# Two strips of heads on TensorE, scores two groups at a time, q's stacked copies held back, low parts on VectorE, in a cross-attention and MoE block

## The chip, the cores and the metric

The kernel runs on one core of one Trainium2 chip. The metric is the device time of one execution in microseconds (us), taken as the median of a few executions.

## The reference

Sixteen batch elements of 128 tokens, width 128. Cut to what matters:

```python
x = x + attention(layernorm(x), ctx, ctx)       # 16 heads of 8 dimensions
x = x + moe(layernorm(x))
# attention: q, k, v = projections with biases
scores = q @ k.T / sqrt(8) + m[h] * softplus(1000 + |i - j|)     # a slope m per head
out    = softmax(scores) @ v, then the projection Wo and its bias
# moe: router softmax over 16 experts, top 2; gated experts of 64 features and a shared one of 128
y = sum_e c_e * (silu(x @ Wg_e) * (x @ Wu_e)) @ Wd_e + shared(x)
```

## The kernel before

**Tiling.** Work goes by groups of two batch elements (b = 0, 1), eight groups in all (NG = 8). Everything of a group has its tokens in 128 partitions or its features there. TensorE, ScalarE, VectorE and GpSimd each have their own instruction order, written out by hand, with semaphores between them; SyncE issues most DMAs.

**Stages.** `first()` does the attention of group 0. Then come seven steps, `step(f, a, p, q, abuf)`: the experts of group f, the attention of group a = f+1, the q and k projections of p = f+2 and the first norm of q = f+3. Steps 1 to 4 are a loop. Each step has a first part and a `second_half`. The experts of the last group stand behind the steps. Inside a step, pieces of the two halves are interleaved: nine chunks `up(f, c)` (six products each), nine chunks `late_down` of the group before, the scores and the values.

**Stacked heads.** To have near-float32 scores from float16 products, q and k are each split into a high float16 part and a low one (`qk_parts`). ScalarE writes the high part (`qk_high`, L714), then a full float32 copy (`qk_copy`, L718); GpSimd subtracts the two (`qk_low`, L1308). In group 0 VectorE makes the low part straight from PSUM instead (`qk_low_first`, L949). SyncE writes the parts to DRAM (L217 to L221) and reads them back as stacks (L229, L235): for each head, 32 rows of `stacks_sb` hold k's and q's parts so that one product over them gives high x high, high x low and low x high together. Rows 96 and 97 hold the shift (below) against ones. The rows between are zeros, filled at the start (L1182, L1195 on VectorE, L860 on ScalarE). A product of scores takes 96 rows, one of transposed scores 98.

**Scores and the shift.** Heads go in four groups g of four, one PSUM bank each. `scores(a, b, g)` (L360) fills the bank `ps_s[g % 2]`; VectorE takes each row's largest value per head (`row_max`, L966), splits it into float16 halves (`nsplit`, L972, L976); TensorE turns it (`shift_T`, L369), ScalarE copies it (`nmT`, L724) and issues the small DMA that writes it into the q stack (`shift_rows`, L741). `scores_T(a, b, g)` (L415) then gives transposed scores minus the maximum in `ps_st`, ScalarE takes the exponential (L730), and `weigh_values` (L434) multiplies by the values. The bias of the slopes is either a product of `dist16` with slope matrices (L378, L383) or a copy of `bias_T` put in the bank ahead (`seed_first` on ScalarE, L737; `seed` on VectorE, L985).

**Which waits matter.** `scores` waits for the maximum two groups back, `scores_T` for the exponential two groups back, and with b = 0 or 1 and g = 0 for the shift rows' DMA. `up(f, 0)` ends with two products on `x2_lo` (L1023 on VectorE, from `x2_hi` of ScalarE, L767). The lines of the change:

```python
# L355: pe.wait_ge(max_sb, n - 1)            scores: the maximum two groups back
# L406: pe.wait_ge(exp_sb, n - 1)            scores_T: the exponential two groups back
# ScalarE, a step: norm2(f,1) qk_high(p,1) x2_high(f) qk_copy(p,1) qk_high(p,0) tanh(f,0) qk_copy(p,0) ...
#   ... tanh(f,3) exponential(a,0,0) shift_copy(a,1) shift_rows(a,1) exponential(a,0,1) tanh(f,4) ...
# VectorE, a step: row_max 0, 1; gate, hidden (f-1, 8); x2_low(f); row_max 2, 3; max_high; gate(f,0); max_low ...
```

Of the kernel before, what the change touches and what calls it, by code (L numbers as in the profile page):

```python
# [17 lines left out]
F32 = mybir.dt.float32  # L18
# [7 lines left out]
P = 128  # L26
# [14 lines left out]
SMALL_SLOPES = 4  # L41
SROWS = 4 * DH
ZROWS = 96
AROWS = ZROWS + 2
# [24 lines left out]
def xattn_moe_kernel(nc, x, ctxT, wqkvoT, bqk, bv, bo, wgT, wuT, wd, wr, c_ident, c_dist, c_select, out):  # L69
# [8 lines left out]
    with stack:  # L78
# [35 lines left out]
        qk_parts, qk_full = sb("qk_parts", [P, 2, 2, T], F16), sb("qk_full", [P, 2, T])  # L114
        stacks_sb = sb("stacks_sb", [AROWS, 2, 2, H, T], F16)
# [5 lines left out]
        nsplit = sb("nsplit", [P, NB, 2, H], F16)  # L121
# [33 lines left out]
        ps_pv = psum("ps_pv", [P, 512])  # L155
        ps_up = [psum("ps_up0", [P, 2, T]), psum("ps_up1", [P, 2, T])]
# [37 lines left out]
        qkfull_sb = sem("qkfull_sb")  # L194
# [15 lines left out]
        def _(sp):  # L210
            def stacks(p, buf):
# [10 lines left out]
                if at_start(p):  # L222
                    sp.wait_ge(act_pads, 1)
                elif isinstance(p, int) and p == 1:
                    sp.wait_ge(dve_pads, 2)
                sp.wait_ge(s_kd, 32 * p + 32)
                for plane, row in ((2, 0), (3, 2 * DH)):
                    src = bass.AP(qk_dram.tensor, (buf * 5 + plane) * (P * T), [[H * T, 2 * DH], [1, H * T]])
                    sp.dma_start(stacks_sb[row:row + 2 * DH, buf, 1].rearrange("r h t -> r (h t)"), src).then_inc(s_stack, 16)  # L229
                if at_start(p):  # L230
                    sp.wait_ge(dve_pads, 1)
# [20 lines left out]
            def load_more():  # L252
                sp.wait_ge(s_nm[0], 16)
                sp.wait_ge(s_nm[1], 16)
                sp.dma_start(x_all[:, 2 * NB:4 * NB, :], x[:, 2 * NB:4 * NB, :]).then_inc(s_x, 16)
                sp.dma_start(ctx_all[:, 2 * T:4 * T], ctxT[:, 2 * T:4 * T]).then_inc(s_ctx, 16)

            def load_rest():
                sp.wait_ge(s_stack, 128)
# [3 lines left out]
                sp.wait_ge(dve_pads, 3)  # L263
# [30 lines left out]
        def _(pe):  # L294
# [42 lines left out]
            def scores(a, b, g, buf):  # L337

                bank, n = ps_s[g % 2], 2 * NHG * a + NHG * b + g
                if b == 0 and g == 0:
                    pe.wait_ge(s_stack, 64 * a + 64)
                    if at_start(a):
# [3 lines left out]
                        pe.wait_ge(dve_pads, 1)  # L348
                        pe.wait_ge(act_pads, 1)
                    elif isinstance(a, int) and a == 1:  # L350
                        pe.wait_ge(act_pads, 3)
                elif b == 0 and g == 1:
                    pe.wait_ge(v_sb, a + 1)
                else:
                    pe.wait_ge(max_sb, n - 1)  # L355
                if g == 0:
                    mm(bank[:], dist16[:], slope_hi[:, 0:HG, :], start=True, stop=False, skip_group_check=True)
                for h in range(HG * g, HG * g + HG):
                    o = (h - HG * g) * P
                    last = mm(bank[:, o:o + P], qs[buf][0:ZROWS, h, b * P:(b + 1) * P],  # L360
                              ks[buf][0:ZROWS, h, b * P:(b + 1) * P],
                              start=(g > 0), stop=True, skip_group_check=True)
                last.then_inc(s_mm, 1)
# [243 lines left out]
            def second_half(f, a, p, q, abuf):  # L607
# [5 lines left out]
                if not at_start(f): down(f - 1, (8,), abuf)  # L613
# [784 lines left out]
```

## Time and profile before

| | |
|---|---|
| median of 3 runs | 248.25 us (247.99 to 249.17) |
| profiled execution | 249.56 us, its span 247.8 us |
| busy: TensorE products, weight loads | 216.5 us, 177.5 us |
| busy: VectorE, ScalarE, GpSimd | 172.4 us, 124.9 us, 83.4 us |
| granted TensorE clock | full, but for 0.67 on average from 27 to 42.5 us |

The times add to more than the span since the engines work side by side. The profiled execution is 249.56 us long by the device's clock, 1.8 us more than its span. A step starts at 42.25, 66.35, then about every 26 us; the steps end at about 226 us.

### The profile page before, as it was taken

How to read it: one execution, taken by the hardware profiler on the slowest of the kernel's cores; microseconds unless marked ns; L12 is line 12 of the kernel's file. 1: busy time of each engine (PE TensorE's matmuls, PEld its weight loads, DVE VectorE, ACT ScalarE, POOL GpSimd, SP SyncE). 2: the span in 40 equal slices, each digit the busy share in tenths (PEclk: the TensorE clock that was granted, in tenths of full speed). 3: DMA queues.
4: the chain of work that ended last, by engine and by line, in shares of the span. 5: the costliest groups of instructions: out<-in, count | busy, mean ns of one | idle time of the engine just before them, and what ended most of it. 6: DMA issues, size and time to landing. Idle time of an engine off the chain costs nothing.

```text
span 247.8 us, 6092 instructions
## 1 busy us (share of the span) xinstructions
PE 216.5 (87%) x1937; PEld 177.5 (72%) x1937; DVE 172.4 (70%) x600; ACT 124.9 (50%) x298; POOL 83.4 (34%) x192
## 2 busy tenths in 40 slices
PE   2978588878989698989999899979997989989995
PEld 2666346666779577967798688957895779768985
DVE  4689614796789556993698478856885589654882
ACT  8475543656454545356446534655545424644320
POOL 2501012501483118610791059114830182018100
PEclk9999957999999999999999999999999999999999
DMA  5553582163303460156106510734044500170000
GB/s 152 169 90 118 107 296 79 36 105 101 75 3 98 69 173 0 42 105 162 31 3 138 144 48 1 136 91 105 3 116 90 132 1 4 26 171 0 0 25 21
DMA packets 13079, 20.24 MB, mean 82 GB/s; under 512 B 2800, under 2 KB 9440, under 8 KB 12544
## 3 DMA queue, kind: packets, MB, share of 16 engines
q1 hardware_dynamic: 12080, 18.64, 31.3%
q10 hardware_dynamic: 976, 1.32, 1.9%
q8 instruction: 12, 0.20, 0.3%
q14 instruction: 11, 0.09, 0.1%
HBM read 16.03 MB, written 3.78 MB: 80 GB/s over the span
## 4 chain that ended last, share of the span: by engine, by line
PE 35%; issue 32%; POOL 13%; DMA 7%; DVE 6%; ACT 5%; ACTq 0%; POOLq 0%; SPq 0%; DVEq 0%
PE ps_up L501 7%; POOL hid L1315 6%; PE ps_m L527 6%; DMA stacks_sb<-nmT 6%; PE ps_pv L434 4%; PE ps_up L506 3%; PE ps_pv L441 2%; PE ps_st L415 2%; DVE nmax L966 2%; PE ps_s L360 2%; DVE stacks_sb L1195 1%; DMA ident<-in_c_ident 1%; POOL qk_parts L1308 1%; PE ps_st L469 1%; PE ps_m L456 1%
## 5 line engine op out<-in xcount | busy, mean ns | idle before, releaser
L730 ACT ACTIVATE probs<-ps_st 128x512 f32<-128x512 f32 x64 | 37.8, 594 | 27.4 <-PE ps_st L415 27.2
L786 ACT ACTIVATE th<-ps_up 128x256 f32<-128x256 f32 x72 | 27.6, 383 | 35.6 <-PE ps_up L506 35.4
L527 PE MATMUL ps_m<-wd_sb,hid 128*128 128x128 f32 x288 | 44.2, 281 | 0.0
L1070 DVE SCALAR_TENSOR_TENSOR tg<-th,ps_up 128x256 f32<-128x256 f32 x72 | 29.8, 414 | 20.2 <-ACT th L786 19.7
L966 DVE TENSOR_REDUCE nmax<-ps_s 128x4 f32<-128x512 f32 x64 | 41.9, 679 | 0.5 <-issue 0.4
L1315 POOL TENSOR_TENSOR hid<-hid,crep 128x256 f32<-128x256 f32 x56 | 39.0, 729 | 5.2 <-ACT x2n L760 3.4
L527 PEld LDWEIGHTS ps_m<-wd_sb,hid 128*128 128x128 f32 x288 | 37.7, 191 | 0.6
L415 PE MATMUL ps_st<-stacks_sb 98*128 98x128 f16 x256 | 25.7, 225 | 9.5 <-DMA stacks_sb<-nmT 6.7
L1076 DVE TENSOR_TENSOR hid<-tg,ps_up 128x256 f32<-128x256 f32 x72 | 29.7, 412 | 1.0
L1271 POOL TENSOR_TENSOR ve<-mv,eps_sb 128x1 f32<-128x1 f32 x16 | 3.0, 189 | 79.6 <-DVE mv L1017 79.6
L415 PEld LDWEIGHTS ps_st<-stacks_sb 98*128 98x128 f16 x256 | 17.9, 100 | 15.6 <-DVE ps_st L985 6.3
L501 PE MATMUL ps_up<-x_hi,wg_hi 128*128 128x256 f32 x72 | 26.6, 369 | 2.5 <-ACT x_hi L767 2.4
L360 PE MATMUL ps_s<-stacks_sb 96*128 96x128 f16 x256 | 23.7, 219 | 0.7 <-DVE nmax L966 0.7
L360 PEld LDWEIGHTS ps_s<-stacks_sb 96*128 96x128 f16 x256 | 17.8, 98 | 4.6 <-DVE nmax L966 1.6
L506 PE MATMUL ps_up<-x_lo,wg_hi 128*128 128x256 f32 x72 | 20.3, 282 | 0.0
L501 PE MATMUL ps_up<-x_hi,wu_hi 128*128 128x256 f32 x72 | 20.3, 282 | 0.0
L501 PE MATMUL ps_up<-x_hi,wu_lo 128*128 128x256 f32 x72 | 20.3, 282 | 0.0
L501 PE MATMUL ps_up<-x_hi,wg_lo 128*128 128x256 f32 x72 | 20.2, 280 | 0.0
L506 PE MATMUL ps_up<-x_lo,wu_hi 128*128 128x256 f32 x72 | 20.1, 280 | 0.0
L434 PE MATMUL ps_pv<-probs,v_aug 128*32 128x384 f32 (+1 forms) x256 | 18.9, 416 | 0.5 <-ACT probs L730 0.5
L1263 POOL TENSOR_TENSOR ve<-mv,eps_sb 128x2 f32<-128x2 f32 x8 | 1.6, 194 | 46.6 <-DVE mv L934 46.6
L501 PEld LDWEIGHTS ps_up<-x_hi,wg_hi 128*128 128x128 f32 x72 | 13.7, 190 | 4.8 <-issue 1.9
(149 smaller groups left out, 447.4 us busy)
## 6 DMA issues: line engine op xcount, KB each, us to landing
crep<-cw_dram SPq DMA_DIRECT2D x28, 256.0 KB, 4.4
stacks_sb<-qk_dram SPq DMA_DIRECT2D x32, 128.0 KB, 4.0
qk_dram<-qk_parts SPq DMA_DIRECT2D x16, 128.0 KB, 1.8
out_y<-x_all SPq DMA_DIRECT2D x8, 128.0 KB, 4.4
wg_sb<-in_wgT ACTq DMA_DIRECT2D x1, 576.0 KB, 3.5
wu_sb<-in_wuT ACTq DMA_DIRECT2D x1, 576.0 KB, 3.3
wd_sb<-in_wd SPq DMA_DIRECT2D x1, 576.0 KB, 4.7
x_all<-in_x SPq DMA_DIRECT2D x2, 256.0 KB, 3.5
```

The costliest lines, as they stand in the source:

```text
L360: last = mm(bank[:, o:o + P], qs[buf][0:ZROWS, h, b * P:(b + 1) * P], ks[buf][0:ZROWS, h, b * P:(b + 1) * P], start=(g > 0), stop=True, sk ...
L415: last = mm(bank[:, o:o + P], ks[buf][:, h, b * P:(b + 1) * P], qs[buf][:, h, b * P:(b + 1) * P], start=first, stop=True, skip_group_check ...
L434: last = mm(ps_pv[32 * c:32 * c + 32, r * 3 * P:(r * 3 + n) * P], v_aug[:, b, r, c, :], probs[:, b, h * P:(h + n) * P], start=True, stop=T ...
L501: mm(ps_up[c % 2][:, k, :], w[:, c, :], x2_hi[:], start=(k == 0 and n == 0), stop=False, skip_group_check=True)
L506: last = mm(ps_up[c % 2][:, k, :], hi[:, c, :], x2_lo[:], start=False, stop=True, skip_group_check=True)
L527: last = mm(ps_dn[:, b * P:(b + 1) * P], hid[:, buf, c, b * P:(b + 1) * P], wd_sb[:, c, :], start=(c == 0 and b == 0), stop=(c == SHARED), ...
L730: fn(probs[:, b, g * HG * P:(g + 1) * HG * P], ps_st[(g + 1) % 2][:], ACT.Exp).then_inc(exp_sb, 1)
L786: fn(th[:, c % 2, :], ps_up[c % 2][:, 0, :], ACT.Tanh, scale=0.5).then_inc(tanh_sb, 1)
L966: v.tensor_reduce(nmax[:, b, HG * g:HG * g + HG], ps_s[g % 2][:].rearrange("p (h j) -> p h j", h=HG), AX_X, ALU.max, negate=True).then_inc ...
L1070: v.scalar_tensor_tensor(out=tg[:, c % 2, :], in0=th[:, c % 2, :], scalar=1.0, in1=ps_up[c % 2][:, 0, :], op0=ALU.add, op1=ALU.mult).then_ ...
L1076: v.tensor_tensor(hid[:, buf, c, :], tg[:, c % 2, :], ps_up[c % 2][:, 1, :], ALU.mult).then_inc(hid_sb, 1)
L1315: g.tensor_tensor(hid[:, buf, c, :], hid[:, buf, c, :], crep[:, c, :], ALU.mult).then_inc(hc_sb, 1)
```

## The change

- **Strips.** The stack has two strips of rows, 0 to 33 and 64 to 97: heads 0 to 7 in the first, heads 8 to 15 in the second. There are no rows of zeros and so no fills. A product of scores takes 32 rows, one of transposed scores 34.
- **Pairs.** A call of `scores` or `scores_T` does two groups of heads, one from each strip, in alternation, into the two banks. It waits for both banks (maximum or exponential `n`, not `n - 1`). The order of groups is 0, 2, 1, 3.
- **Seeds.** In group 0 all biases of `scores_T` are products; later one seed on ScalarE and two on VectorE, all into one bank.
- **Low parts.** `qk_copy` and GpSimd's `qk_low` go; VectorE makes the low parts from PSUM, around `x2_low`, and waits until both high parts are there.
- **DMAs.** Each stack copy and each copy of shift rows is two DMAs, one per strip. SyncE waits for the shift rows of b = 1 before it issues q's stack copies.
- **Order.** `down(f-1, 2)` stands ahead of `up(f, 0)`, `down(f-1, 8)` behind the values of b = 0; ScalarE's copy of the values stands behind two exponentials; GpSimd doesn't wait for `x2n` before it weighs experts.

```diff
 # rows
+STRIP = 64
-ZROWS = 96
-AROWS = ZROWS + 2
+AROWS = SROWS + 2
+HS = H // 2
+ORDER = (0, 2, 1, 3)
 # SyncE, stacks(p)
                 sp.wait_ge(s_qd, 16 * p + 16)
+                if not at_start(p):
+
+                    sp.wait_ge(s_nm[1], 32 * p)
                 for row in (0, 2 * DH):
-                    src = bass.AP(qk_dram.tensor, buf * 5 * (P * T), [[H * T, 2 * DH], [1, H * T]])
-                    sp.dma_start(stacks_sb[row:row + 2 * DH, buf, 0].rearrange("r h t -> r (h t)"), src).then_inc(s_stack, 16)
+                    for s in range(2):
+                        src = bass.AP(qk_dram.tensor, (buf * 5 * P + s * HS) * T, [[H * T, 2 * DH], [1, HS * T]])
+                        at = STRIP * s + row
+                        sp.dma_start(stacks_sb[at:at + 2 * DH, buf, 0].rearrange("r h t -> r (h t)"), src).then_inc(s_stack, 16)
 # TensorE, scores(a, b, j)
+                    pe.wait_ge(max_sb, n)
+                for k in range(HG):
+                    for s in range(2):
+                        row, h = STRIP * s, HG * j + k
+                        last = mm(ps_s[s][:, k * P:(k + 1) * P], qs[buf][row:row + SROWS, h, b * P:(b + 1) * P],
+                                  ks[buf][row:row + SROWS, h, b * P:(b + 1) * P], start=(j > 0 or s > 0), stop=True,
+                                  skip_group_check=True)
+                        if k == HG - 1:
+                            last.then_inc(s_mm, 1)
 # TensorE, scores_T(a, b, j)
+                seeded = not at_start(a) and (b, j) != (0, 1)
...
+                if not (at_start(a) and b == 0 and j == 0):
+                    pe.wait_ge(exp_sb, n)
...
+                for k in range(HG):
+                    for s in range(2):
+                        row, h = STRIP * s, HG * j + k
+                        last = mm(scores_bank(a, 2 * j + s)[:, k * P:(k + 1) * P], ks[buf][row:row + AROWS, h, b * P:(b + 1) * P],
+                                  qs[buf][row:row + AROWS, h, b * P:(b + 1) * P], start=first[s], stop=True,
+                                  skip_group_check=True)
 # TensorE, a step
                 scores(a, 0, 0, abuf)
-                scores(a, 0, 1, abuf)
...
                 late_down(0)
-                scores(a, 0, 2, abuf)
                 late_down(1)
                 expert_in_T(f)
-                scores(a, 0, 3, abuf)
+                scores(a, 0, 1, abuf)
+                late_down(2)
                 up(f, 0)
-                late_down(2)
+                up(f, 1)
                 scores(a, 1, 0, abuf)
...
-                scores_T(a, 0, 0, abuf)
+                scores_T(a, 0, 0, abuf, f=f)
                 late_down(6)
                 shift_T(a, 1)
-                scores_T(a, 0, 1, abuf, f=f)
                 late_down(7)
...
                 up(f, 4)
-                scores_T(a, 0, 2, abuf)
+                scores_T(a, 0, 1, abuf)
                 weights_T(f, a)
-                scores_T(a, 0, 3, abuf)
                 up(f, 5)
-                if not at_start(f): down(f - 1, (8,), abuf)
                 scores_T(a, 1, 0, abuf)
                 weigh_values(a, 0, f)
+                if not at_start(f): down(f - 1, (8,), abuf)
                 scores_T(a, 1, 1, abuf)
                 values_T(a, 0)
-                scores_T(a, 1, 2, abuf)
 # TensorE, first()
+                scores_T(0, 0, 0, 0)
                 shift_T(0, 1)
-                keep_clock(2)
-                scores_T(0, 0, 0, 0)
                 scores_T(0, 0, 1, 0)
 # ScalarE
-                    act.wait_ge(qkfull_sb, 2 * p)
+                    act.wait_ge(qklo_sb, 2 * p + 2)
...
                 act.wait_ge(nm_sb, 2 * a + b + 1)
-                act.dma_start(qs[buf][ZROWS:AROWS, :, b * P:(b + 1) * P], nmT[:, b, :]).then_inc(s_nm[b], 16)
+                for s in range(2):
+                    act.dma_start(qs[buf][STRIP * s + SROWS:STRIP * s + AROWS, :, b * P:(b + 1) * P],
+                                  nmT[H * s:H * (s + 1), b, :]).then_inc(s_nm[b], 16)
 # ScalarE, a step
                 shift_copy(a, 1)
                 shift_rows(a, 1, abuf)
+                exponential(a, 0, 1)
...
                 exponential(a, 1, 0)
+                exponential(a, 1, 1)
                 values_copy(a, 0)
-                exponential(a, 1, 1)
 # VectorE
+            def qk_low(p, k):
+                if at_start(p):
+                    dve.wait_ge(qkhi_sb, 2 - k)
+                else:
+                    dve.wait_ge(qkhi_sb, 2 * p + 2)
...
+                bank = ps_k0 if k and at_start(p) else ps_qk[:, k * T:(k + 1) * T]
                 v.scalar_tensor_tensor(out=qk_parts[:, k, 1, :], in0=bank, scalar=bqk_sb[:, k:k + 1],
                                        in1=qk_parts[:, k, 0, :], op0=ALU.add, op1=ALU.subtract).then_inc(qklo_sb, 1)
 # VectorE, a step
+                if p is not None: qk_low(p, 1)
                 x2_low(f)
+                if p is not None: qk_low(p, 0)
                 row_max(a, 0, 2)
 # VectorE and ScalarE, at the start
-            v.memset(stacks_sb[:, 0, 0].bitcast(F32), 0.0).then_inc(dve_pads, 1)
-            v.memset(stacks_sb[:, 1].bitcast(F32), 0.0).then_inc(dve_pads, 1)
-            fill(stacks_sb[:, 0, 1], zero)
+            for s in range(2):
+                fill(ks[0][STRIP * s + SROWS:STRIP * s + AROWS], ones16)
 # GpSimd, a step
-                    pool.wait_ge(x2n_sb, NB * f + NB)
...
-                    qk_low(p, 1)
-                    qk_low(p, 0)
```

## Rows read from the trace of the kernel before

**Rows 1.** The page: its span and the busy time of each engine

```profile
span 247.8 us, 6092 instructions
...
PE 216.5 (87%) x1937; PEld 177.5 (72%) x1937; DVE 172.4 (70%) x600; ACT 124.9 (50%) x298; POOL 83.4 (34%) x192
```

**Rows 2.** The chain that ended last, step 3: start us, us, what

```profile
120.37 0.45 PE ps_s L360 x8
...
137.03 1.04 PE ps_pv L434 x16
```

**Rows 3.** TensorE in order of time, step 3, first part

```profile
123.89 0.38 PE L501 MATMUL ps_up<-x_hi,wg_hi 128*128 128x256 f32 x1 [0.41 <-ACT x_hi L767]
...
126.38 0.40 PE L360 MATMUL ps_s<-stacks_sb 96*128 96x128 f16 x4
126.71 0.23 PE L369 MATMUL ps_pv<-ident,nsplit 128*32 128x128 f16 x1
126.87 0.28 PE L469 MATMUL ps_st<-wr_hi,x_lo 128*128 128x16 f32 x1
```

**Rows 4.** VectorE in order of time: the start, and step 3

```profile
10.21 0.48 DVE L949 SCALAR_TENSOR_TENSOR qk_parts<-ps_st,bqk_sb,qk_parts 128x256 f16<-128x256 f32 x1 [1.20 <-ACT qk_parts L705]
...
12.90 3.47 DVE L1195 MEMSET stacks_sb<- 98x4096 f32 x1 [0.80 <-issue]
...
123.90 0.42 DVE L1023 TENSOR_TENSOR x_lo<-ps_st,x_hi 128x256 fp32r<-128x256 f32 x1 [0.51 <-ACT x_hi L767]
124.24 1.28 DVE L966 TENSOR_REDUCE nmax<-ps_s 128x4 f32<-128x512 f32 x2
```

**Rows 5.** ScalarE in order of time, step 3

```profile
123.38 0.38 ACT L767 ACTIVATE x_hi<-ps_st 128x256 fp32r<-128x256 f32 x1 [0.25 <-PE ps_st L462]
123.66 0.47 ACT L718 ACTIVATE qk_full<-ps_st,bqk_sb 128x256 f32<-128x256 f32 x1
...
132.05 0.27 ACT L724 ACTIVATE nmT<-ps_pv 32x128 f16<-32x128 f16 x1
132.35 0.62 ACTq L741 DMA_DIRECT2D stacks_sb<-nmT  x1
133.08 0.60 ACT L730 ACTIVATE probs<-ps_st 128x512 f32<-128x512 f32 x1 [0.77 <-PE ps_st L415]
...
134.87 0.36 ACT L779 ACTIVATE cwT<-ps_pv 16x256 f32<-16x256 f32 x1
```

**Rows 6.** TensorE in order of time: scores_T and what stands by it, four stages

```profile
27.12 0.40 PE L415 MATMUL ps_st<-stacks_sb 98*128 98x128 f16 x4 [1.35 <-ACT ps_st L737]
...
30.18 0.61 PE L415 MATMUL ps_st<-stacks_sb 98*128 98x128 f16 x4 [0.97 <-DVE ps_st L985]
...
52.95 0.38 PE L415 MATMUL ps_st<-stacks_sb 98*128 98x128 f16 x4 [1.22 <-DMA stacks_sb<-nmT]
...
57.28 0.40 PE L415 MATMUL ps_st<-stacks_sb 98*128 98x128 f16 x4 [0.38 <-DVE ps_st L985]
...
130.97 0.39 PE L415 MATMUL ps_st<-stacks_sb 98*128 98x128 f16 x4
...
131.78 0.23 PE L369 MATMUL ps_pv<-ident,nsplit 128*32 128x128 f16 x1
...
132.34 0.39 PE L415 MATMUL ps_st<-stacks_sb 98*128 98x128 f16 x4
...
136.65 0.38 PE L415 MATMUL ps_st<-stacks_sb 98*128 98x128 f16 x4 [0.66 <-DMA stacks_sb<-nmT]
...
145.75 0.38 PE L357 MATMUL ps_s<-slope_hi,dist 128*128 128x512 f16 x1
...
209.17 0.39 PE L415 MATMUL ps_st<-stacks_sb 98*128 98x128 f16 x4
...
214.14 0.40 PE L415 MATMUL ps_st<-stacks_sb 98*128 98x128 f16 x4
```

**Rows 7.** Waits over the whole run: us in total, times, longest us

```profile
PE ps_st L415 <- DMA stacks_sb<-nmT: 6.7, 6, 1.6
```

More of the change, by code:

```diff
@@ L335, in project_v, with scores @@
                 last.then_inc(v_mm, 1)
[L337 to L343, printed above, removed]
+            def scores(a, b, j, buf):
+                n = 2 * NHG * a + NHG * b + 2 * j
+                if b == 0 and j == 0:
+                    pe.wait_ge(s_stack, 128 * a + 128)
+                    pe.wait_ge(v_sb, a + 1)
                     if at_start(a):
@@ L347, in scores @@
                         pe.wait_ge(own, 6)
[L348 to L353, printed above, removed]
-                else:
[L355 to L363, printed above, removed]
+                else:
+                    pe.wait_ge(max_sb, n)
+                if j == 0:
+                    mm(ps_s[0][:], dist16[:], slope_hi[:, 0:HG, :], start=True, stop=False, skip_group_check=True)
+                for k in range(HG):
[6 more added lines that the diff above has]
+                            last.then_inc(s_mm, 1)
             def shift_T(a, b):
@@ L411, in scores_T @@
                         pe.wait_ge(act_pads, 2)
-                first = False if seeded else bias(bank, g)[0]
-                for h in range(HG * g, HG * g + HG):
-                    o = (h - HG * g) * P
-                    last = mm(bank[:, o:o + P], ks[buf][:, h, b * P:(b + 1) * P], qs[buf][:, h, b * P:(b + 1) * P],
-                              start=first, stop=True, skip_group_check=True)
-                    first = False
-                last.then_inc(st_mm, 1)
+                    elif isinstance(a, int) and a == 1:
+                        pe.wait_ge(act_pads, 4)
+                first = [False if seeded else bias(scores_bank(a, 2 * j), ORDER[2 * j])[0],
+                         bias(scores_bank(a, 2 * j + 1), ORDER[2 * j + 1])[0]]
+                for k in range(HG):
[4 more added lines that the diff above has]
+                                  skip_group_check=True)
+                        first[s] = False
+                        if k == HG - 1:
+                            last.then_inc(st_mm, 1)
             def weigh_values(a, b, f=None):
@@ L532, in first @@
                 scores(0, 0, 0, 0)
-                scores(0, 0, 1, 0)
                 keep_clock(1)
@@ L884, in _ @@
             fn(wr_hi[:], wr_sb[:], ACT.Copy).then_inc(act_setup, 1)
-            act.wait_ge(s_stack, 64)
+            act.wait_ge(s_stack, 128)
             act.dma_start(wu_sb[:], wuT).then_inc(s_wu, 16)
-            act.wait_ge(dve_pads, 2)
-            fill(ks[1][ZROWS:AROWS], ones16)
+            for s in range(2):
+                fill(ks[1][STRIP * s + SROWS:STRIP * s + AROWS], ones16)
             first()
@@ L1093, in first @@
                 max_low(0, 0)
-                for g in range(NHG):
-                    row_max(0, 1, g)
+                row_max(0, 1, 0)
+                row_max(0, 1, 1)
+                qk_low(1, 1)
+                qk_low(1, 0)
+                row_max(0, 1, 2)
+                row_max(0, 1, 3)
                 max_high(0, 1)
@@ L1138, in step @@
                 hidden(f, 2, 1 - abuf)
+                row_max(a, 1, 2)
                 row_max(a, 1, 3)
@@ L1158, in second_half @@
                 seed(a, 0)
-                seed(a, 1)
                 gate(f, 5)
@@ L1162, in second_half @@
                 hidden(f, 5, 1 - abuf)
+                seed(a, 1)
                 if not at_start(f): residual2(f - 1)
@@ L1342, in _ @@
             pool.wait_ge(zero_sb, 1)
-            inverse_deviation1(0)
+            step(None, None, None, 0, 0)
             pool.wait_ge(rstd1_sb, 1)
```

143 lines of the change are left out of this document (53 added, 90 removed).

## The prediction

> **What bounds the kernel now.** I read the page first: TensorE is busy for 216.5 of 247.8 us, the other engines far less [rows 1]. That makes it the first suspect, but a busy TensorE is not a full one, so I read its own order of time through step 3, and beside it those of VectorE and ScalarE in the same window. TensorE is in order; what counts is each place where it waits, and on whom. In a step there are few: for `x2_hi` ahead of the first `up` (0.41 us), and for the shift rows of b = 1 ahead of `scores_T(a, 1, 0)` (0.66) [rows 3, 6]. The wait list puts all waits of `scores_T` for that small DMA at 6.7 us in six times [rows 7]; 1.22 of it is in step 0 [rows 6], so steps 1 to 5 lose about 1.1 each. All the rest of a step is TensorE's own sequence. The change touches both: it packs products, and it rearranges what the waits hang on.
>
> **The pairs on TensorE.** Eight products of 96 rows take 0.45 us, 0.056 each, so four take 0.22 [rows 2]. If the two strips work side by side, a pair call has four slots: 0.22 instead of 0.45. That tiles can work side by side, the values show: 16 products on strips of 32 columns move 8 x 384 + 8 x 128 = 4096 columns in 1.04 us [rows 2], 0.25 ns a column in float32, where the untiled float16 products take 56/128 = 0.44. But a switch between tiled and untiled isn't free. `shift_T` is one product with 32 columns: the four ahead of it start at 126.38 and should be over at 126.60, it starts at 126.71, and what follows it starts at 126.87, 0.10 later than one product would need [rows 3]. So in and out cost 0.11 + 0.10 = 0.21, and a pair call is 0.43, against 0.45 now. All 8 calls of a step together win less than 0.2 us, in places where TensorE will wait anyway; I count 0. The bounds for strips of rows, which this trace doesn't show: no switch cost (a call is 0.22) and no overlap (0.66). I take 0.43, since strips of columns on this same engine are the nearest row for both.
>
> The Trainium skill's TensorEngine Tiling (Array Packing), Theoretical Speedup, has up to 2x for a dimension of at most 64, and its Key Properties say that changing the mode drains TensorE. The gaps by `shift_T` agree with the second; by the first alone, the eight calls of a step would save 8 x 0.22 = 1.8 us and seven steps 12.
>
> **First part of a step: VectorE gets later.** Now `x2_low` starts at 123.90, right behind `x2_hi`, and `row_max` 2 and 3 at 124.24 [rows 4]. With the change `qk_low(p, 1)` stands ahead of it and waits for both high parts; that of q is made on ScalarE only behind `x2_hi`, in the slot of the copy at 123.66, and takes 0.47: ready at 124.13 [rows 5]. `qk_low` at 0.48 [rows 4] (its group-0 form, the same operation) gives 124.6, `x2_low` at 0.42 is ready at 125.03, 0.7 later than today. The last two products of `up(f, 0)` need it. TensorE, which has filled its gap with `down(f-1, 2)` and so starts `up(f, 0)` near 123.95, stands some 0.5. The second `qk_low` (0.4 in sequence) puts `row_max` 2 and 3 at 125.35 to 126.6, 1.1 later. `scores(a, 1, 0)` needs both maxima now, TensorE waits again, then `shift_T(a, 0)` for the halves of the maximum: it comes near 127.4 instead of 126.71. From there to `scores_T(a, 0, 0)` the sequence is the same work, **+0.7 a step** where p exists (bounds: 0 if the two waits are absorbed, +1.1). What leaves GpSimd (two `qk_low`) and ScalarE (two copies) was hidden work: 0. That GpSimd weighs earlier lets `down(f-1, 2)` stand ahead of `up`: in this sum already.
>
> **Second part: a chain through ScalarE.** X is the start of `scores_T(a, 0, 0)`. Today the next exponential needs one bank, and TensorE runs ahead: `scores_T(a, 0, 2)` goes in without a wait. Now `scores_T(a, 0, 1)` needs both exponentials, and the second stands on ScalarE behind `shift_copy(a, 1)` and two DMA issues. Step by step: the call is 0.17 (a bias product of three heads) + 0.43; `down` 6 and `shift_T` follow as now, where `shift_T` is 131.78 - 130.97 - 0.22 = 0.6 behind its quad [rows 6], so it starts at X + 1.2; the copy starts 0.27 later (131.78 to 132.05) and takes 0.27, and one issue 0.62 [rows 5, 6]; two issues X + 3.0; the exponential waits out the issue, as at 133.08 (0.1), 0.6 [rows 5]: X + 3.7. Then `scores_T(a, 0, 1)`: bias 0.40 (131.94 to 132.34 [rows 6]), then the tiled products, 0.26 to their last start and some 0.25 to ScalarE; two exponentials of 0.57 and between them the weights' copy 0.3 (0.36 as recorded [rows 5]). So `scores_T(a, 1, 0)` can start at about **X + 6.1**. It waits for both exponentials as well. TensorE stands some 1.1 us before the first of them and 0.6 before the second; `up(f, 4)`, `up(f, 5)` and the weights' turning are its cover, and used up. Behind ScalarE's issues queue the exponential and `tanh(f, 4)`.
>
> Today that distance is 136.65 - 130.97 = 5.68 in step 3, and with the mean wait of 1.1 instead of 0.66 it is 6.1 in steps 1 to 5; 4.33 in step 0 (57.28 - 52.95) and 4.97 in step 6 (214.14 - 209.17) [rows 6, 7]. So holding back q's copies removes a wait for the DMA, and the chain takes its place: **0 in steps 1 to 5**. In step 0 there is no `down` 6, the chain is 5.6: **+1.3**. In step 6, **+1.1**. The second issue is bounded by 0 and 0.62 (each has half the rows to write); I take 0.62, its own line's.
>
> From `scores_T(a, 1, 0)` to the next step it is 9.1 us now (145.75 - 136.65) [rows 6]. `down(f-1, 8)` moves in (0.44), the values' wait for their copy goes (about 0.4), and the second seed, behind `gate`, `norm1` and `hidden`, holds `scores_T(a, 1, 1)` by some 0.2: +0.1. Held q copies start when the shift rows have landed and have 9 us until the next step: hidden. SyncE's `cw_dram` and `crep` issues queue behind them and come some 3 us later; their cover is the time to the next step's weighing.
>
> **The start.** The fills go, 3.47 us of it on VectorE [rows 4]. But it ran while the stacks were on their way, and pairs take turns with `row_max`: TensorE waits for two maxima, VectorE for two banks, some 0.6 between each two. That gives back what the fill frees: 0. Then today's four `scores_T` follow each other, 3.06 us from 27.12 to 30.18 [rows 6]. Now `shift_T(0, 1)` stands behind the first pair, and exponentials behind its copy and two issues: the chain as above without `down` and weights' copy, 5.2, with more bias products (all of group 0) 5.7. **+2.6**; the seed on ScalarE that goes (its end set 27.12) is about paid by the second issue for b = 0.
>
> **Sum.** Start 2.6; step 0: first part 0.5 (part of its 0.7 lies beside the 1.22 wait for the DMA) + 1.3 + 0.1 = 1.9; steps 1 to 5: 5 x (0.7 + 0 + 0.1) = 4.0; step 6: no `qk_low`, the moved `down` gives back 0.2, + 1.1 + 0.1 = 1.0. Together 9.5 us. The span is then 257.3. The profiled execution is at 249.56, 0.5% over the median of 248.25; on the median the sum gives **257.7 us**.
>
> **Rivals.**
> - *The hold pays (faster).* If the chain from X is short, the wait for shift rows is simply gone. TensorE's own work from X to `scores_T(a, 1, 0)` is 5.68 - 0.66 - 0.44 = 4.6 (less the wait there and the moved `down`). The chain stands in seven steps and the start, so each 0.1 of it is 0.8 in all; it decides from X + 4.9, 1.2 below my sum. At 4.6: 257.7 - 8 x 1.5 = **245.7 us**. For it: the DMA waits are real. Against it: exponential, issue and copy have measured lengths. 0.15.
> - *Row strips switch freely.* Five of the eight calls of a step lie on the path, each 0.2 shorter, 7.0 in seven steps, 0.6 at the start: **250 us** (247.5 to 252). Nothing in the trace speaks for it but that these are other strips than the values'. 0.2.
> - *No overlap.* Two strips, or their weight loads, go one after the other: + 0.22 in each of five to eight calls, 8 to 12 us: **268**. Against it: the values' strips overlap. 0.12. The skill's TensorE: Matmul & The Clock Gate, Measured speedup vs the span model, has 3.07x for four row strips at 512 columns; in proportion a pair would be 0.29 instead of 0.22, 2 to 4 us more than my sum. No row here shows it.
> - *My forecast* with its own bounds (second issue short: -4; first part 0 to 1.1): 252 to 262. 0.53.
>
> **Range and chances.** 247.5 to 265 leaves out the faster case and most of the slowest. A difference under 0.5% (1.2 us) is what a measurement of this kernel can't tell from none. Faster 0.15; within it half of the free switch, 0.1; slower 0.75.
>
> **What would show it.** After: `scores_T` pairs in 0.22 with gaps of 0.1 on both sides (free: no gaps; no overlap: 0.45); `x2_low` behind a `qk_low` near 1.1 us after `x2_hi` starts; waits of `scores_T` and its weight loads put down to exponentials instead of the DMA; two issues of 0.6 in a row on ScalarE; X to `scores_T(a, 1, 0)` near 6.1 in every step. The forecast is wrong if that distance is under 5, if `scores` pairs have no gaps, or if step 0's `scores_T(1, 0, 0)` comes before 55, two behind 52.95.

## The result, and the profile after

The changed kernel takes 263.2 us (262.35 to 264.45, 4 runs) against 248.71 us (4 runs): ratio 1.057, interval 1.050 to 1.065. It is slower by 14.5 us, the forecast had 9.5. Here and below, a ratio leaves out executions of either kernel that were disturbed, so it need not be the quotient of the two medians. Its profiled execution is at 262.74, with a span of 260.9. The page: span, TensorE's busy time, and TensorE's granted clock in 40 slices:

```profile
span 260.9 us, 6137 instructions
...
PE 222.8 (85%) x1946; PEld 166.1 (64%) x1946; DVE 174.2 (67%) x610; ACT 117.9 (45%) x284; POOL 74.2 (28%) x178
...
PEclk9999755685899999999999999999999999999999
```

TensorE is busy for 6 us more, the span is 13.1 us longer [rows 1]. The clock stands at 5 and 6 in several slices between 33 and 65 us. Two stretches of the windows view, after; the columns are length, busy time (instructions) of TensorE, its weight loads, VectorE, ScalarE and GpSimd, then the granted clock, DMA share and GB/s:

```profile
27.00:47.00 20.00, 13.84 (x86) 7.05 (x86) 4.20 (x20) 6.29 (x13) 2.17 (x6) 0.56 0.44 138
47.00:72.00 25.00, 22.43 (x176) 15.09 (x175) 17.36 (x61) 13.07 (x31) 3.23 (x10) 0.74 0.29 79
```

The same two of the kernel before:

```profile
27.00:47.00 20.00, 16.15 (x118) 10.40 (x118) 8.46 (x32) 9.97 (x22) 5.15 (x15) 0.74 0.46 136
47.00:72.00 25.00, 22.01 (x206) 17.75 (x207) 19.22 (x72) 13.75 (x36) 7.31 (x18) 1.00 0.34 78
```

So here is a difference that the prediction has no term for: a mean clock of 0.56 instead of 0.74, then 0.74 instead of 1.00. From 72 us on both run at 1.00.

TensorE in step 3, after, in order of time (start, us, engine, line, operation, count, and in brackets the idle time before it and who ended it):

```profile
129.62 0.39 PE L358 MATMUL ps_s<-slope_hi,dist 128*128 128x512 f16 x1
129.94 0.40 PE L362 MATMUL ps_s<-stacks_sb 32*128 32x128 f16 x8
130.27 0.70 PE L323 MATMUL ps_st<-xnT,wT 128*128 128x256 f32 x2
...
134.73 0.39 PE L518 MATMUL ps_up<-x_lo,wg_hi 128*128 128x256 f32 x1 [0.44 <-DVE x_lo L1015]
...
136.32 0.39 PE L358 MATMUL ps_s<-slope_hi,dist 128*128 128x512 f16 x1 [0.38 <-DVE nmax L957]
...
141.18 0.33 PE L386 MATMUL ps_st<-slope_small,dist 128*128 128x384 bf16 x1
...
145.02 0.34 PE L381 MATMUL ps_st<-slope_hi,dist 128*128 128x384 f16 x1 [1.02 <-ACT probs L720]
...
147.36 0.32 PE L386 MATMUL ps_st<-slope_small,dist 128*128 128x384 bf16 x1 [0.43 <-DVE ps_st L977]
...
156.39 0.38 PE L358 MATMUL ps_s<-slope_hi,dist 128*128 128x512 f16 x1
```

The pair of scores: bias at 129.62, eight tiled products from 129.94, next instruction 130.27. Narrow windows on this stretch show that the eight start in four couples, at 129.94, 130.01, 130.06 and 130.12, so a slot is 0.06 and the four are over near 130.18. The next instruction comes some 0.1 after that (the way out). From the start of the bias product to the next one it is 0.22 at 119.99 in the kernel before and 0.32 here, 0.1 more on the way in. The pair's 0.43 of the forecast is 0.43 to 0.44. In the first part of the step the wait for `x_lo` is 0.44, for the two maxima 0.38 (before: 0.41 for `x2_hi` [rows 3], and none for the maxima, at 125.16). In the second part X, the start of `scores_T(a, 0, 0)`, is 141.18; the second pair waits 1.02 for an exponential, the third pair (147.36) 0.43 for VectorE's seed. X to the third pair is 6.18 (forecast 6.1), where it was 5.68 [rows 6]; in step 6 it is 6.11, in step 0 6.96. The waits over the whole run say it in two lines:

```profile
PE ps_st L381 <- ACT probs L720: 11.9, 10, 2.8
...
PE ps_st L386 <- DVE ps_st L977: 2.6, 6, 0.4
```

No wait of `scores_T` for the DMA is left; 6.7 us of it were there [rows 7]. The chain took its place. VectorE in step 3, after, in order of time:

```profile
133.86 0.48 DVE L939 SCALAR_TENSOR_TENSOR qk_parts<-ps_st,bqk_sb,qk_parts 128x256 f16<-128x256 f32 x1 [0.94 <-ACT qk_parts L707]
134.26 0.41 DVE L1015 TENSOR_TENSOR x_lo<-ps_st,x_hi 128x256 fp32r<-128x256 f32 x1
134.60 0.47 DVE L939 SCALAR_TENSOR_TENSOR qk_parts<-ps_st,bqk_sb,qk_parts 128x256 f16<-128x256 f32 x1
134.99 1.28 DVE L957 TENSOR_REDUCE nmax<-ps_s 128x4 f32<-128x512 f32 x2
```

ScalarE in step 3, after, in order of time:

```profile
142.68 0.27 ACT L713 ACTIVATE nmT<-ps_pv 32x128 f16<-32x128 f16 x1
142.97 1.28 ACTq L732 DMA_DIRECT2D stacks_sb<-nmT  x2
144.36 0.60 ACT L720 ACTIVATE probs<-ps_st 128x512 f32<-128x512 f32 x1 [1.42 <-issue]
...
145.93 0.60 ACT L720 ACTIVATE probs<-ps_st 128x512 f32<-128x512 f32 x1 [0.70 <-PE ps_st L425]
```

`x_lo` comes behind a `qk_low` [rows 4], and two issues of the shift rows take 1.28 on ScalarE, one took 0.62 [rows 5]: the second costs full price, though each writes half the rows. The exponential waits them out.

The start on TensorE, after: the second, third and fourth pair, and the first product of step 0:

```profile
29.29 0.45 PE L381 MATMUL ps_st<-slope_hi,dist 128*128 128x384 f16 x1 [2.80 <-ACT probs L720]
...
31.89 0.61 PE L381 MATMUL ps_st<-slope_hi,dist 128*128 128x512 f16 x1 [1.17 <-ACT probs L720]
...
36.85 0.50 PE L381 MATMUL ps_st<-slope_hi,dist 128*128 128x384 f16 x1 [1.21 <-ACT probs L720]
...
46.99 0.63 PE L358 MATMUL ps_s<-slope_hi,dist 128*128 128x512 f16 x1
```

Step 0 starts at 46.99, 4.7 later than before (42.25). The same span, divided at step starts (each the bias product of `scores(a, 0, 0)`):

| | before | after | grew | forecast |
|---|---|---|---|---|
| start, to step 0 | 42.25 | 46.99 | 4.7 | 2.6 |
| step 0 | 24.1 | 27.7 | 3.6 | 1.9 |
| steps 1 to 5, mean of one | 26.4 | 27.2 | 0.8 | 0.8 |
| step 6 and the rest | 49.5 | 50.4 | 0.9 | 1.0 |

The steps came as summed. The miss, 3.8 us, stands where the clock was low.

### The profile page after: what moved, and what is told of

The parts are those of the page before. It is cut to its first block, busy times and chain, and to the rows that moved or that the text cites. A ratio compares the mean times of both kernels' runs of the same rounds, so it can differ in the third digit from the quotient of the medians.

```text
span 260.9 us, 6137 instructions
## 1 busy us (share of the span) xinstructions
PE 222.8 (85%) x1946; PEld 166.1 (64%) x1946; DVE 174.2 (67%) x610; ACT 117.9 (45%) x284; POOL 74.2 (28%) x178
## 3 DMA queue, kind: packets, MB, share of 16 engines
q1 hardware_dynamic: 13104, 18.64, 26.2%
## 4 chain that ended last, share of the span: by engine, by line
PE 39%; issue 31%; POOL 10%; DVE 9%; ACT 6%; ACTq 3%; DMA 1%; DVEq 0%; POOLq 0%; SPq 0%
PE ps_m L539 7%; POOL hid L1301 5%; PE ps_up L513 5%; PE ps_pv L446 5%; DVE nmax L957 3%; ACT probs L720 3%; PE ps_st L425 3%; PE ps_pv L453 2%; ACTq L732 2%; PE ps_up L308 2%; PE ps_up L518 2%; PE ps_st L381 2%; PE ps_st L481 1%; DMA ident<-in_c_ident 1%; PE ps_st L386 1%
## 5 line engine op out<-in xcount | busy, mean ns | idle before, releaser
L720 ACT ACTIVATE probs<-ps_st 128x512 f32<-128x512 f32 x64 | 36.2, 593 | 31.4 <-PE ps_st L425 20.3
L539 PE MATMUL ps_m<-wd_sb,hid 128*128 128x128 f32 x288 | 45.5, 289 | 0.0
L957 DVE TENSOR_REDUCE nmax<-ps_s 128x4 f32<-128x512 f32 x64 | 40.9, 681 | 1.4 <-PE ps_s L362 0.9
L539 PEld LDWEIGHTS ps_m<-wd_sb,hid 128*128 128x128 f32 x288 | 37.1, 190 | 4.3 <-DVE hid L1068 0.8
L518 PE MATMUL ps_up<-x_lo,wg_hi 128*128 128x256 f32 x72 | 21.3, 296 | 2.5 <-DVE x_lo L1015 2.5
L518 PEld LDWEIGHTS ps_up<-x_lo,wg_hi 128*128 128x128 f32 x72 | 14.0, 194 | 3.7 <-DVE x_lo L1015 3.7
L381 PE MATMUL ps_st<-slope_hi,dist 128*128 128x384 f16 (+1 forms) x11 | 4.5, 405 | 12.7 <-ACT probs L720 11.9
L982 DVE RECIPROCAL rden<-ps_pv 128x16 f32<-128x16 f32 x16 | 4.1, 258 | 16.8 <-PE ps_pv L453 16.4
L308 PE MATMUL ps_up<-ident 128*128 128x128 f32 x73 | 11.2, 297 | 4.6 <-DMA ident<-in_c_ident 4.6
```

Of the source, the lines that this page charges most:

```text
L308: nc.tensor.transpose(ps_up[1][:, 0, 0:P] if bank is None else bank, ident[:], ident[:])
L381: last = mm(bank[:, 0:n_split * P], dist16[:], part[:, h0:h0 + n_split, :], start=first, stop=False, skip_group_check=True)
L518: last = mm(ps_up[c % 2][:, k, :], hi[:, c, :], x2_lo[:], start=False, stop=True, skip_group_check=True)
L539: last = mm(ps_dn[:, b * P:(b + 1) * P], hid[:, buf, c, b * P:(b + 1) * P], wd_sb[:, c, :], start=(c == 0 and b == 0), stop=(c == SHARED), ...
L720: fn(probs[:, b, g * HG * P:(g + 1) * HG * P], scores_bank(a, i)[:], ACT.Exp).then_inc(exp_sb, 1)
L957: v.tensor_reduce(nmax[:, b, HG * g:HG * g + HG], ps_s[i % 2][:].rearrange("p (h j) -> p h j", h=HG), AX_X, ALU.max, negate=True).then_inc ...
```

## The experiments

Ratios are against the kernel before on the same chip. That kernel stood at 247.99 us beside experiments 1 to 4, 247.36 beside 5, 6, 7 and 9, and 249.02 beside 8, 10, 11 and 12. The theory after the result: (a) in the steps, ScalarE's issues and VectorE's low parts set the pace; (b) in the start and step 0, the half clock does. Rivals: the tiled products themselves are slow; a DMA wait is hidden somewhere; the layout is bad in itself.

**1. Exponential ahead of the issues.**

```diff
 # ScalarE, step
                 exponential(a, 0, 0)
+                exponential(a, 0, 1)
                 shift_copy(a, 1)
                 shift_rows(a, 1, abuf)
-                exponential(a, 0, 1)
```

> The changed kernel with one edit: in a step ScalarE takes the second exponential of b = 0 ahead of the shift's copy and its two DMA issues. Chain theory (the two issues in front of that exponential hold the second pair of transposed scores): the pair starts without its wait of 1.02 us, the next one 4.9 to 5.3 us behind X instead of 6.18, the time falls by 6 to 9 us to 254 to 257. Rival (TensorE's work or the shift rows' DMA is what counts): the wait comes back ahead of the third pair as a wait for that DMA, since it is issued 0.6 us later, and the time stays within 2 us of 263.

Measured 258.13 us (255.94 to 261.03), ratio 1.046 (1.036 to 1.056): 5 us less than the changed kernel, a little short of what the chain theory asked (254 to 257). TensorE, step 3: X and the third pair:

```profile
137.47 0.33 PE L386 MATMUL ps_st<-slope_small,dist 128*128 128x384 bf16 x1
...
140.12 0.34 PE L381 MATMUL ps_st<-slope_hi,dist 128*128 128x384 f16 x1
...
142.91 0.34 PE L386 MATMUL ps_st<-slope_small,dist 128*128 128x384 bf16 x1 [0.87 <-DVE ps_st L977]
```

The second pair no longer waits; X to the third pair is 5.44 instead of 6.18, just above the 4.9 to 5.3 expected. The seed on VectorE is the next wait (0.87). Steps 3 to 5 take 26.2 each instead of 27.0. Part of the 5 us in the whole is not this edit: step 0 starts at 44.62 here although the start's code is the same (more below).

**2. Low parts behind the maxima.**

```diff
 # VectorE, step
-                if p is not None: qk_low(p, 1)
                 x2_low(f)
-                if p is not None: qk_low(p, 0)
 ...
                 max_low(a, 0)
+                if p is not None:
+                    qk_low(p, 1)
+                    qk_low(p, 0)
```

> The changed kernel with one edit: VectorE makes x2's low part first, then the maxima 2 and 3, and q's and k's low parts only behind the halves of the maximum. Theory that the order on VectorE costs the first part of a step 0.7 us where there is a next group: the wait of 0.44 us in up 0 and the one ahead of the scores of b = 1 go, first part from 12.0 to 11.3 us, six steps, 259 to 260. Rival (the low parts are late for the DRAM round trip and the seeds, so it is paid later): within 1 us of 263.

Measured 258.0 us (256.99 to 260.51), ratio 1.045 (1.036 to 1.054), below the 259 to 260 expected. TensorE, step 3: step start, X, `shift_T(a, 1)`, third pair:

```profile
125.04 0.39 PE L358 MATMUL ps_s<-slope_hi,dist 128*128 128x512 f16 x1
...
135.93 0.33 PE L386 MATMUL ps_st<-slope_small,dist 128*128 128x384 bf16 x1
...
137.48 0.23 PE L372 MATMUL ps_pv<-ident,nsplit 128*32 128x128 f16 x1 [0.26 <-DVE nsplit L967]
...
142.44 0.32 PE L386 MATMUL ps_st<-slope_small,dist 128*128 128x384 bf16 x1 [0.43 <-DVE ps_st L977]
```

Start to X is 10.89 instead of 11.56: the 0.7 of the forecast's first part comes back. But VectorE is late later: `shift_T` waits 0.26 for the split maximum, and X to the third pair grows from 6.18 to 6.51. Net 0.4 a step. Again part of the total is the clock (step 0 starts at 44.57 instead of 46.99).

**3. Idle products in the start's waits.**

```diff
 # TensorE, first
                 shift_T(0, 1)
+                keep_clock(24)
                 scores_T(0, 0, 1, 0)
+                keep_clock(10)
                 scores_T(0, 1, 0, 0)
 ...     # 10, 6 and 5 more before scores_T(0,1,1,0) and the two attention_T
```

> The changed kernel with 55 more idle products on TensorE in the waits of the first group (24, 10, 10, 6 and 5), so that it is never idle for long there. Clock theory: the granted clock stays at 2.4 GHz from 27 to 67 us; step 0 starts near 44 instead of 46.99 and takes 25.5 instead of 27.7 us, the time falls by 4 to 6 us to 257 to 259. Rival (the start is long by its waits alone, at either clock): step 0 starts within 0.7 us of 46.99 and the time stays within 2.5 us.

Measured 257.78 us (256.93 to 262.84), ratio 1.041 (1.034 to 1.049). Its profiled execution was the slowest of the five, with two later falls of the clock; only its start is read here. TensorE's first, second and third pair, and step 0:

```profile
24.86 0.38 PE L381 MATMUL ps_st<-slope_hi,dist 128*128 128x512 f16 x1 [0.82 <-issue]
...
28.90 0.34 PE L381 MATMUL ps_st<-slope_hi,dist 128*128 128x384 f16 x1
...
30.95 0.39 PE L381 MATMUL ps_st<-slope_hi,dist 128*128 128x512 f16 x1
...
40.87 0.38 PE L358 MATMUL ps_s<-slope_hi,dist 128*128 128x512 f16 x1
```

The clock is 1.00 from 27 to 43 us, and step 0 starts at 40.87, 6.1 us earlier than in the changed kernel and 1.4 earlier than in the kernel before at its half clock. The products write nothing that is read. So the half clock was worth 6 us in the start alone, and TensorE had been slow in work that lay on the path. The second pair stands 4.04 behind the first in both kernels (28.90 - 24.86; 29.29 - 25.25): the chain through ScalarE is the same as ever. The other half of the expectation, step 0 at full clock in 25.5 us, did not come true: the clock stood at 0.50 from 51 to 55 us and step 0 took 27.9 (40.87 to 68.72).

**4. One strip after the other.** The rival that tiled products don't overlap as ordered:

```diff
 # scores and scores_T
-                for k in range(HG):
-                    for s in range(2):
+                for s in range(2):
+                    for k in range(HG):
```

> The changed kernel with one edit: in a pair the four products of the first strip go before the four of the second, so that neighbours are in the same strip. If strips overlap only when they alternate, a pair takes 0.45 us instead of 0.22 between its gaps; with five to eight of the eight calls on the path, 1.1 to 1.8 us a step, 271 to 275. Rival: most calls stand ahead of a wait and the time moves by under 3 us. If the queue overlaps them in either order: 263, with 0.22 us in the trace.

Measured 263.37 us (262.66 to 264.19), ratio 1.064 (1.057 to 1.071): as the changed kernel. TensorE, step 3:

```profile
130.01 0.41 PE L362 MATMUL ps_s<-stacks_sb 32*128 32x128 f16 x8
```

Eight products with four of one strip first still take 0.41 (0.40 in alternation, row 129.94 above), and the next instruction starts 0.33 behind them in both. Narrow windows show four couples here too, at 130.01, 130.08, 130.13 and 130.19. Order doesn't matter, and the tiled products are not where the time went.

**5. No hold.**

```diff
 # SyncE, stacks(p), ahead of q's copies
-                if not at_start(p):
-
-                    sp.wait_ge(s_nm[1], 32 * p)
```

> The changed kernel without the wait that holds back q's stack copies. In the changed kernel the chain through ScalarE, 6.18 us behind X, ends later than the shift rows land. If the hold hides a real wait, the shift rows of b = 1, issued 3.1 us behind X, land some 4.2 us later (as 132.35 to 136.51 before), 7.3 behind X: the third pair then waits for the DMA, + 1.1 us a step in six steps, 268 to 270. If SyncE's copies are through before those rows are issued (they now start 7 us before X, since the low parts are made early), nothing waits: 263.

Measured 261.7 us (261.06 to 266.84), ratio 1.052 (1.043 to 1.061). SyncE in step 3, in order of time:

```profile
137.88 2.22 SPq L239 DMA_DIRECT2D stacks_sb<-qk_dram  x4
```

TensorE in the same step, second and third pair:

```profile
144.47 0.34 PE L378 MATMUL ps_st<-slope_hi,dist 128*128 128x384 f16 x1 [1.02 <-ACT probs L717]
...
146.82 0.32 PE L383 MATMUL ps_st<-slope_small,dist 128*128 128x384 bf16 x1 [0.43 <-DVE ps_st L974]
```

q's copies are issued from 137.88, and the shift rows of b = 1 at 142.43 on ScalarE. The DMA engines' busy share is 0.50 from 140 to 141 us, 0.01 from 141 to 142 and 0.00 from 142 to 143, so the copies are through by then. The two transfers don't meet, and the two waits are those of the changed kernel, 1.02 and 0.43. So the hold hides nothing there. By the trace the DMA wait is gone because VectorE makes the low parts some 4 us earlier in the step than GpSimd did (first write of the parts 4.8 us behind the step's start, 134.42 - 129.62; before, at 129.11, it was 9.1 behind). The prediction had put this to the hold. That the low parts' place is the cause is argued from these times; no run moved them alone.

**6. The second strip's rows issued by SyncE.**

```diff
 # ScalarE, shift_rows(a, b)
-                for s in range(2):
+                for s in range(2 - b):
 # SyncE, ahead of the hold
+                    second_strip(p - 1, 1 - buf)     # waits nm_sb, one dma_start of nmT[H:2H, 1]
```

> The changed kernel with one edit: the second of the two DMAs with shift rows of b = 1 is issued by SyncE. Chain theory: the exponential behind the issues starts 0.65 us earlier, so the wait of the second pair falls from 1.02 to 0.4 us and the third pair stands 5.5 us behind X: 0.65 in seven steps, 258 to 259. Rival (the seed on VectorE ends last ahead of the third pair in either case): a wait of the third pair for the seed grows by what the second lost and the time falls by under 2 us.

Measured 260.57 us (259.08 to 262.23), ratio 1.052 (1.043 to 1.060). TensorE, step 3:

```profile
143.41 0.34 PE L387 MATMUL ps_st<-slope_hi,dist 128*128 128x384 f16 x1 [0.36 <-ACT probs L726]
...
145.75 0.32 PE L392 MATMUL ps_st<-slope_small,dist 128*128 128x384 bf16 x1 [0.43 <-DVE ps_st L983]
```

The total was expected at 258 to 259. The second pair waits 0.36 instead of 1.02, less by the 0.64 of one issue; steps 3 to 5 take 26.3 each instead of 27.0. In its profiled execution the clock fell to half once more, from 107 to 114 us, and that step took 30.0. So the total shows less than the other steps gained.

**7. The three together** (1, 2 and 3).

> The changed kernel with the edits of the first three experiments together: second exponential ahead of the shift's DMA issues, low parts of q and k behind the maxima, idle products in the start. By the single edits, 0.7 and 0.4 us a step in seven and six steps and 5 us of clock: 263.2 - 4.9 - 2.4 - 5 = 251. If the edits take the place of one another's waits: 253 to 256. It is above the kernel before in either case, since the switches and the pair waits stay.

Measured 247.1 us (246.13 to 247.84, 10 runs), ratio 0.997 (0.993 to 1.001): level with the kernel before, better than the 251 and the 253 to 256 expected. Steps 1 to 5 take 25.7 each, step 0 starts at 40.93. TensorE's third pair of step 3 waits for the seed:

```profile
135.30 0.34 PE L386 MATMUL ps_st<-slope_small,dist 128*128 128x384 bf16 x1 [0.64 <-DVE ps_st L982]
```

**8. All five edits** (7, with 6, and the seed ahead of `hidden(f, 4)` on VectorE).

> Edit: e6_three_edits with the second strip's shift rows of b=1 issued by SyncE (as in e7_issue_sync) and the bias seed of the third pair put ahead of hidden(f,4) on VectorE. Theory: in e6 the second pair no longer waits for a DMA (exponential(a,0,1) hides it), so the second issue on ScalarE costs there only what it delays tanh and the exponential behind it (0.64 of ScalarE), and the third pair waits 0.64 for the seed, of which moving it gives 0.3: 0.3 to 0.7 per step over six steps, 243 to 245, level with b1. Rival, that the chain has passed to VectorE's or ScalarE's sum of work: within 1 us of e6, 246 to 247.5.

Measured 245.75 us (244.43 to 246.33), ratio 0.987 (0.982 to 0.992), against 243 to 245 expected. The wait for the seed fell from 0.64 to 0.42 in step 3, but a step takes 25.6 on average against 25.7: less than the 0.3 to 0.7 that I expected. Taking the second issue off ScalarE gave nothing here, since in 7 the second pair didn't wait any more; the two edits that relieve one wait don't add. (The issue and the seed were moved together, so this is read from the waits.) About 1 us of the 1.4 us in span against 7 is step 0, 25.15 instead of 26.2, where the clock's fall was shorter. The one execution whose mean clock was 1.00 took 244.43, the other five 245.68 to 246.33.

**9. The kernel before, with the hold alone.**

```diff
 # SyncE, stacks(p), kernel before, ahead of q's copies
+                if not at_start(p):
+                    sp.wait_ge(s_nm[1], 16 * p)
```

> The kernel before with one part of the change alone: SyncE waits for the shift rows of b = 1 before it issues q's stack copies. The wait of transposed scores for that DMA (0.66 to 1.55 us in steps 1 to 5) should go; what ends next is the seed and the product down 8, 4.9 to 5.2 us behind X against 6.1: 0.9 to 1.2 in five steps, 242 to 244. Rival (the rows are late because of k's copies, which are not held, or because small DMAs into the stack take 4 us anyway): the wait stays and the time is 248.

Measured 244.23 us (242.02 to 244.6), ratio 0.981 (0.973 to 0.989): faster than before by 1.9% (1.3% by the two medians; both ends of the interval are below 1). A step of 1 to 5 takes 25.4 us instead of 26.4. The one part of the change that pays does so where the copies really collide. The waits:

```profile
PE ps_st L417 <- DMA stacks_sb<-nmT: 1.3, 2, 1.1
```

**10. The hold at the wrong rows** (`s_nm[0]`, those of b = 0).

> Edit: as b1_before_hold, but SyncE waits for the first b's shift rows (s_nm[0]) instead of the second's. These land before q's stacked copies are ready to be issued (before: first rows issued some 6 us ahead of them; second rows at 132.35, copies at 132.16). Theory that b1 gains because the 8 KB of the second b's rows no longer stand behind 256 KB of q's copies in the DMA engines: the copies go out as before, the wait of scores_T for DMA returns (6 waits, 6.7 us), and the time is that of before, 247.0 to 248.5. Rival, that any wait on SyncE ahead of the copies shifts its later transfers favourably: as b1, near 244.

Measured 247.36 us (246.36 to 249.03, 10 runs), ratio 0.998 (0.994 to 1.002). SyncE in step 3, q's copies:

```profile
130.44 0.76 SPq L237 DMA_DIRECT2D stacks_sb<-qk_dram  x2
```

The waits of `scores_T` for the DMA, over the whole run:

```profile
PE ps_st L417 <- DMA stacks_sb<-nmT: 4.5, 5, 1.2
```

q's copies start at 130.44 and the shift rows are issued at 130.54, as close as before (132.16 and 132.35 [rows 5]); most of the wait is back. With the right rows (9) the copies started 2.9 us behind the issue (133.04 and 130.17), and `scores_T(a, 1, 0)`, the first call that needs the rows, started at 133.78 without a wait for them, 3.6 behind the issue. So it is the order of these two transfers that pays, not a pause on SyncE. The chain of the kernel before has the transfer's length, from its issue, with the copies ahead of it:

```profile
132.35 4.17 DMA stacks_sb<-nmT
```

**11. The kernel before, with idle products alone** (10, 9, 4, 4 and 5 in the start's waits).

> Edit: the kernel before with those 32 idle products alone, without the hold. Theory: as above, 2 us less than before, some 245.5 to 246.5; with b1's 4 us this adds up to b2. Rival, that hold and clock are one thing (b1's gain would be a gain of clock): then this one gives nothing or b2 no more than b1.

Measured 245.08 us (243.84 to 245.98), ratio 0.984 (0.979 to 0.989). TensorE's first and fifth call of `scores_T` and its first product of step 0:

```profile
26.74 0.40 PE L415 MATMUL ps_st<-stacks_sb 98*128 98x128 f16 x4 [0.26 <-ACT ps_st L741]
...
29.81 0.40 PE L415 MATMUL ps_st<-stacks_sb 98*128 98x128 f16 x4
...
38.28 0.38 PE L357 MATMUL ps_s<-slope_hi,dist 128*128 128x512 f16 x1
```

Step 0 starts 4.0 us earlier than 42.25, at a clock of 1.00 throughout. I had expected half of that: TensorE bounds the start more than I thought.

**12. Hold and idle products in the kernel before.**

> Edit: the kernel before, with SyncE's wait for the second b's shift rows ahead of q's stacked copies (as in b1_before_hold) and with 10, 9, 4, 4 and 5 more idle products in TensorE's waits of the start (ahead of scores_T(0,0,0), scores_T(0,1,0), attention_T(0,0), weigh_values(0,1), attention_T(0,1)). Theory that the half clock after 31 us is what the start's sparse work costs: in the kernel before the clock is .50 from 31 to 39, and the work of that stretch takes about 4 us less at the full clock if it is bound by TensorE, less where it waits for ScalarE; step 0 starts at 39 to 40 instead of 41.9, and the kernel takes 241.5 to 242.5 against b1's 244.2. Rival, that the start before is bound by exponentials and not by TensorE: within 0.5 of b1.

Measured 240.86 us (239.81 to 242.21), ratio 0.967 (0.962 to 0.973), a little below the 241.5 to 242.5 expected. The two gains add (0.981 x 0.984 = 0.965), so they are two things. This is the fastest version: 3.3% under the kernel before, 8.5% under the changed one (240.86 / 263.2). Its page:

```profile
span 239.8 us, 6163 instructions
...
PEclk9999999999999999999999999999999999999999
```

Against 8, the best of the strips: steps 1 to 5 take 25.6 us in both, the rest behind step 6's start 49.5 and 49.3. The difference of 4.1 us in span is the start (38.20 and 41.54) and step 0 (24.1 and 25.15). So in the steps the version with strips and its edits is level with the one without; in the start, and in step 0 with its fall of the clock, it costs.

## Why the prediction was right, and where it was off

- **What bounds the kernel: held.** The pace of a step is TensorE's sequence plus a few waits, and each edit that shortened one wait (1, 2, 6) shortened the step by what the trace showed for it, less what was late next.
- **The pair at 0.43: held** (0.44), and with it two rivals fell: switches aren't free, and there is overlap, in either order (4). The four slots take 0.22 to 0.24: the fourth couple starts 0.18 behind the first. The 0.29 in proportion to the Trainium skill's TensorE: Matmul & The Clock Gate, Measured speedup vs the span model, is not seen here. The drain at a change of mode, which TensorEngine Tiling (Array Packing) of the Trainium skill states under Key Properties, agrees with the 0.1 on each side. As the mechanism says, the strips give nothing in a step: 25.6 us with and without (8, 12), though those two differ in more than the strips.
- **First part + 0.7: held.** Step start to X is 11.56 in step 3 against 10.98 (130.97 [rows 6] - 119.99), so + 0.6, and 2 brings it down by 0.67, to 10.89.
- **The chain of 6.1: held** (6.18 in step 3), and its parts: two issues 1.28, where I had taken 0.62 each. 1 and 6 take the chain apart at the exponential and at the issue.
- **"Holding back q's copies removes a wait for the DMA": right that the wait goes, wrong why.** It goes without the hold as well (5). By the trace it is the low parts' new place that keeps the two transfers apart; no run moved them alone. The same hold is worth 1.9% in the kernel before (9, 10).
- **Steps 1 to 6: 5.0 forecast, 4.7 measured.**
- **The start + 2.6 and step 0 + 1.9: mis-sized, 4.7 and 3.6.** The sum took every duration at the clock at which the kernel before ran it, and the trace of before had shown that clock falling to half (0.67 on average from 27 to 42.5 us). The new chain leaves TensorE standing 2.80, 1.17, 1.21 and 0.77 us between 26 and 41 us, and the clock stayed at half until about 50 us instead of 40 (0.78 from 49 to 51; 0.85 from 39 to 43). At full clock in both, the start ends at 40.87 (3) and 38.28 (11): 2.6 apart, the forecast's own number, but in part by luck. The first call of `scores_T` starts at 24.86 against 26.74, 1.9 earlier, where the sum had 0 for the seed and the fills. From it to `scores_T(0, 1, 0)` it is 6.09 against 3.07, + 3.0 where the sum had 2.6. From there to step 0 it is 9.92 against 8.47, + 1.45, for which the sum had no term; the likely reason is the fourth pair, which waits 1.21 for an exponential in the changed kernel. The half clock costs the start before 4.0 us (42.25 - 38.28) and the changed one 6.1 (46.99 - 40.87); the 2.1 between are the miss. The term of the start was right in its chain, had errors beside it that nearly cancelled, and lacked the clock.
- **Step 0** has a second stretch at half clock, 0.71 from 55 to 59 and 0.50 to 67 us; the kernel before is at 1.00 there. X to the third pair takes 6.96 in it instead of 6.18. How much of the 1.7 us is the clock isn't settled: 3, 7 and 8, whose start was at full clock, still fell to between 0.5 and 0.7 somewhere from 51 to 59 us, and no run kept step 0 full without other edits.

**The hold-pays rival** (245.7) asked for a short chain; 1, 2 and 3 together made it 5.54 and gave 247.1.

## What to carry to other kernels

Before a saving on the busiest engine is counted, look for where the work lands that used to run ahead: here `scores_T` no longer runs one bank ahead, and each instruction between two exponentials on ScalarE, a DMA issue above all, came onto the path. A sum of durations holds at one clock only: where a change makes TensorE wait in a stretch that already runs low, read the granted clock in windows, and try idle products in the waits first (1.6% here for 32 of them). And where a small transfer is waited for, look at what its neighbours put into the queues just ahead of it: one wait on SyncE gave 1.9%.

## What the runs showed of the hardware that was not expected

- **Tiled products of two strips overlap in any order.** Four of strip 0 and then four of strip 1 take 0.41, in alternation 0.40; from the first start to the next instruction it is 0.33 in both, some 0.1 of it for leaving the mode, against 0.45 for eight untiled ones.
- **Half the rows, the same issue.** ScalarE's issue of shift rows takes 0.64 with 16 rows of `nmT`, 0.62 with 32.
- **The length of a half-clock stretch is not set by the code of the stretch alone.** Three kernels with the same code in the start (the changed one, 1 and 2) begin step 0 at 46.99, 44.62 and 44.57 us; their mean clock from 27 to 47 us is 0.56, 0.74 and 0.74. What decided it is open. Three more, whose start differs in the order of tiles (4), in a wait of SyncE (5) or in who issues one DMA (6), begin it at 46.64, 44.67 and 44.65 with 0.66, 0.74 and 0.66. With idle products in the kernel before (11, 12) the mean clock of the whole run was 1.00 in 11 of 12 executions and 0.998 in the other.
- **A fall can come late.** In 6 the clock fell once in the middle of a full step, at 107 us, and the step took 30.0 instead of 26.6 as the one before it; in 3 the mean clock was 0.55 from 107 to 114 us.
